# Scaling and splitting the attention weights: one scale per half matrix, maxima and the look for low halves on TensorE, and TensorE's program laid out twice

## The reference, cut to what matters

```python
x = x + attn(layernorm(x), wq, bq, wk, bk, wv, bv)   # x: 1 x 2048 x 1024
x = x + ffn(layernorm(x), w1, w2, w3)                # w1, w2: 2752 x 1024; w3: 1024 x 2752

def attn(h, ...):                                    # 32 heads of 32
    q = (h @ wq.T + bq).reshape(B, S, 32, 32)        # k, v alike; wq, wk, wv rounded to 8-bit floats (e4m3)
    scores = einsum('bshd,bstd->bsht', q, k) / sqrt(32)   # heads of one token against each other
    return einsum('bsht,bstd->bshd', softmax(scores), v).reshape(B, S, E)

def ffn(h, w1, w2, w3):
    dq = nf4_quant_dequant                           # blocks of 64, 16 levels
    return (silu(h @ dq(w1).T) * (h @ dq(w2).T)) @ dq(w3).T
```

## Time and profile before

| | us |
|---|---|
| median of 3 runs | 2055.94 (2054.3 to 2056.95) |
| profiled execution | 2054.98 |
| its span, first to last instruction | 2053.2 |

### The profile page before, as it was taken

How to read it: one execution, slowest core, us unless ns; L and a number is a source line. 1 busy time by engine, 2 the same in 40 slices (tenths; PEclk the granted TensorE clock), 3 DMA queues, 4 the chain that set the end, 5 groups by cost and what they waited for, 6 DMA issues and landing times. The chain is left out here.

```text
span 2053.2 us, 30858 instructions
## 1 busy us (share of the span) xinstructions
PE 1977.3 (96%) x10392; PEld 1069.7 (52%) x10392; DVE 1817.0 (88%) x1831; ACT 1466.1 (71%) x1640; POOL 1156.3 (56%) x700
## 2 busy tenths in 40 slices
PE   4699999999998999999999999999999999999998
PEld 3377878777776444444444444444444444444442
DVE  8679898998997899998989999899998989999972
ACT  5524242424256798989889899898998989898872
POOL 0100101010131669787787878878778796887964
PEclk8799999999997999999999999999999999999999
DMA  7114434343324651212122221212121212222114
GB/s 297 62 52 144 138 128 140 116 152 129 116 98 123 200 180 42 62 42 59 44 51 52 46 57 46 57 42 61 41 61 42 61 42 52 50 49 50 38 35 164
DMA packets 219661, 175.65 MB, mean 86 GB/s; under 512 B 143664, under 2 KB 186672, under 8 KB 219568
## 3 DMA queue, kind: packets, MB, share of 16 engines
q1 hardware_dynamic: 219568, 174.62, 29.4%
HBM read 115.34 MB, written 25.17 MB: 68 GB/s over the span
## 5 line engine op out<-in xcount | busy, mean ns | idle before, releaser
L1355 ACT ACTIVATE signs<-w_nat,compare_bias 128x1024 int8<-128x1024 f32 (+2 forms) x896 | 958.9, 1131 | 20.1 <-issue 17.8
L1482 DVE SCALAR_TENSOR_TENSOR bank<-signs,bank 128x1024 f32<-128x1024 int8 (+2 forms) x761 | 926.5, 1218 | 45.1 <-ACT signs L1355 16.4
L1655 PE MATMUL bank<-x2T_hi,w12T_hi 128*128 128x512 f16 x1376 | 521.5, 379 | 1.3 <-DVE w_nat L1499 1.3
L1656 PE MATMUL bank<-x2T_lo,w12T_hi 128*128 128x512 f16 x1376 | 521.5, 379 | 0.0
L1657 PE MATMUL bank<-x2T_hi,w12T_lo 128*128 128x512 f16 x1376 | 521.5, 379 | 0.0
L880 PE MATMUL bank<-wT_hi,xT_hi 128*128 128x512 f16 x768 | 293.0, 381 | 12.4 <-issue 12.4
L880 PE MATMUL bank<-wT_hi,xT_lo 128*128 128x512 f16 x768 | 292.9, 381 | 0.0
L1676 PE MATMUL bank<-w3T_hi,hT_hi 128*128 128x512 f16 x704 | 268.4, 381 | 13.4 <-DVE hidden L1508 7.4
L1677 PE MATMUL bank<-w3T_lo,hT_hi 128*128 128x512 f16 x704 | 267.7, 380 | 0.0
L1678 PE MATMUL bank<-w3T_hi,hT_lo 128*128 128x512 f16 x704 | 267.6, 380 | 0.0
L1283 POOL TENSOR_TENSOR acc<-acc,hidden 128x512 f32<-128x512 f32 x176 | 221.1, 1270 | 47.0 <-ACT hidden L1395 46.1
(11 more groups left out here) (126 smaller groups left out, 2720.6 us busy)
## 6 DMA issues: line engine op xcount, KB each, us to landing
ff_raw<-in_L_ffn_w SPq DMA_DIRECT2D x63, 512.0 KB, 4.5
w_nat<-in_L_ffn_w SPq DMA_DIRECT2D x63, 512.0 KB, 3.9
x_nat<-in_L_attn_hidden_states SPq DMA_DIRECT2D x16, 512.0 KB, 3.7
x_res<-in_L_attn_hidden_states SPq DMA_DIRECT2D x16, 512.0 KB, 4.5
x<-x_res SPq DMA_DIRECT2D x16, 512.0 KB, 2.9
acc<-x SPq DMA_DIRECT2D x4, 2048.0 KB, 8.2
out<-acc SPq DMA_DIRECT2D x16, 512.0 KB, 2.6
w_raw<-in_L_attn_wq SPq DMA_DIRECT2D x8, 512.0 KB, 7.1
```

The costliest lines, as they stand in the source:

```text
L1355: nc.scalar.activation(signs[0:rows, ring(v, k), 0:cols], w_nat[0:rows, v % SLOTS, 0:cols], ACT.Sign, scale=COMPARE[SUMMED[k]][0], bias=co ...
L1482: V.scalar_tensor_tensor(to, part, HALF_STEP[SUMMED[k]], before, ALU.mult, ALU.add).then_inc(sign_used, 1)
L1655: nc.tensor.matmul(dst, hi, x2T_hi[:, toks, c], start=c == 0, stop=False)
L1656: nc.tensor.matmul(dst, hi, x2T_lo[:, toks, c], start=False, stop=False)
```

## The change

The weight stage works by half matrices, six groups of four parts (512 output columns), each with a scale of its own, set one group ahead. The maxima of the parts are shared between VectorE (6 parts) and ScalarE (18 parts; it takes the sum of magnitudes, an upper bound of the maximum). The maximum over partitions is found by turning the column of 128 maxima into a row on TensorE (turn_top), reducing the row on VectorE (set_row), and spreading the two scales back to all partitions by a matmul with ones (spread_row). PSUM is used in three slots of two banks: one transposition unit is eight 128x128 blocks, one high half and one low half instruction has 1024 columns. The low halves are looked at by TensorE: each 128x128 block is multiplied by itself (square_lo, 192 matmuls added up in one bank), and the diagonal is reduced at the end. The residual's first load waits for the first projected half, GpSimd's clearings move into steps 0 and 1 behind 1/std, ScalarE waits for each where it first writes the cleared tile, and x and the biases are loaded after a third of the weights is turned, as before. TensorE's whole program behind the flag, the feed-forward stage included, stands twice: first the one without low halves, which the branch falls into when the flag is zero, then the one with them.

```diff
-                both(attend_tensor, feed_tensor, pe)
+                attend_tensor(pe, feed_tensor)
...
+        GROUPS = 6
+        top = sb("qkv_top", [P, GROUPS])
+        ones = sb("ones", [P, P])
+        scale_row = sb("scale_row", [1, 3, GROUPS])
+        scales = sb("scales", [P, 2, GROUPS])
+        w_scale, un_scale = scales[:, 0], scales[:, 1]
...
-        RING = 4
-        FILLS = C * 2
+        SLOTS = 3
+        PAIRS = C // 2
         PART = C // LOADS
-        LOOKS = {4 + k: k for k in range(LOADS)}
-        SCALE = 13
-        STATS, NORM = 4, 8
+        GROUP_PARTS = LOADS // 2
+        BY_VECTOR = ((0, 2), (0, 2), (3,), (3,), (), ())
+        by_scalar = [(g, j) for g in range(GROUPS) for j in range(GROUP_PARTS) if j not in BY_VECTOR[g]]
+        STATS_GROUP = 4
+        LO_SQUARES = 6
+        TOPS = 7
+        X_TURN = GROUPS * PAIRS % SLOTS * 2
+        def pair_of(n):
+            g, i = divmod(n, PAIRS)
+            m, half = divmod(g, 2)
+            return g, m, (slice(None), m, slice(2 * i, 2 * i + 2), slice(half * BANK, half * BANK + BANK))
+        def pair_banks(n):
+            return bank[:, n % SLOTS * 2:n % SLOTS * 2 + 2]
...
-                sp.wait_ge(w_turned, FILLS)
+                sp.wait_ge(w_turned, 2 * PAIRS)
...
-                for m in range(3):
-                    pool.wait_ge(local_max, m + 1)
-                    nc.gpsimd.partition_all_reduce(top_all[:, m:m + 1], top[:, m:m + 1], P, ALL_MAX).then_inc(global_max, 1)
+
                 inv_std(pool, 0)
-                pool.wait_ge(lo_sum_ready, 1)
-                nc.gpsimd.partition_all_reduce(lo_sum[:, 1:2], lo_sum[:, 0:1], P, ALL_MAX).then_inc(lo_known, 1)
...
+                def look(g):
+                    for j in BY_VECTOR[g]:
+                        wait_part(dve, g, j)
+                        nc.vector.tensor_reduce(part_max[:, g, j:j + 1], part_of(g, j), AX.X, ALU.max,
+                                                apply_absolute_value=True).then_inc(w_seen, 1)
+                def find_top(g):
+                    if BY_VECTOR[g]:
+                        dve.wait_ge(w_seen, sum(len(js) for js in BY_VECTOR[:g + 1]))
+                    dve.wait_ge(w_summed, sum(at <= g for at, _ in by_scalar))
+                    nc.vector.tensor_reduce(top[:, g:g + 1], part_max[:, g], AX.X, ALU.max).then_inc(local_max, 1)
+                def set_row(g):
+                    pow2, w_row, un_row = (scale_row[:, k, g:g + 1] for k in (2, 0, 1))
+                    dve.wait_ge(top_turned, g + 1)
+                    seq.mark(nc.vector.tensor_reduce(pow2, bank[0:1, TOPS, 0:P], AX.X, ALU.max))
                     seq.wait(dve)
+                    seq.mark(nc.vector.tensor_scalar(pow2, pow2, TINY, None, ALU.max))
                     seq.wait(dve)
+                    seq.mark(nc.vector.tensor_scalar(pow2.bitcast(I32), pow2.bitcast(I32), EXPONENT_BITS, None, ALU.bitwise_and))
                     seq.wait(dve)
+                    seq.mark(nc.vector.reciprocal(w_row, pow2))
+                    nc.vector.tensor_scalar(un_row, pow2, 2.0 ** -14 / X_SCALE, None, ALU.mult).then_inc(row_set, 1)
+                    seq.wait(dve)
+                    nc.vector.tensor_scalar(w_row, w_row, 2.0 ** 14, None, ALU.mult).then_inc(row_set, 1)
+                def set_scale(g):
+                    dve.wait_ge(row_spread, g + 1)
+                    nc.vector.tensor_copy(scales[:, :, g], bank[:, TOPS, P + 2 * g:P + 2 * g + 2]).then_inc(scale_set, 1)
+                look(0)
+                find_top(0)
+                set_row(0)
+                set_scale(0)
+                look(1)
+                for n in range(GROUPS * PAIRS):
+                    g, m, dst = pair_of(n)
+                    i = n % PAIRS
+                    if i == 0:
+                        dve.wait_ge(scale_set, g + 1)
+                    dve.wait_ge(w_hi_done, n + 1)
+                    nc.vector.scalar_tensor_tensor(wT_lo[dst], pair_banks(n), w_scale[:, g:g + 1], wT_hi[dst],
+                                                   ALU.mult, ALU.subtract).then_inc(w_lo_done, 1)
+                    if g + 1 < GROUPS and i < 3:
+                        (find_top, set_row, set_scale)[i](g + 1)
+                    if i == 2 and g + 2 < GROUPS:
+                        look(g + 2)
+                    if i == 3 and g == STATS_GROUP - 1:
+                        norm_stats(dve, 0, 0, 1)
+                    if i == 3 and g == STATS_GROUP:
+                        norm_apply(dve, 0, 0)
+                dve.wait_ge(lo_looked, 1)
+                seq.mark(nc.vector.tensor_tensor(lo_squares[:], bank[:, LO_SQUARES, 0:P], ident[:], ALU.mult))
+                seq.wait(dve)
+                nc.vector.tensor_reduce(lo_sum[:, 0:1], lo_squares[:], AX.X, ALU.max).then_inc(lo_sum_ready, 1)
+                dve.wait_ge(lo_added, 1)
+                nc.vector.tensor_copy(lo_sum[0:1, 1:2], bank[0:1, TOPS, 0:1]).then_inc(lo_known, 1)
+                split_lo(dve, 0, xT_lo[:, 0], xT_hi[:, 0], x_hi_done, x_lo_done, X_TURN)
...
-                def look_at_lo(q):
-                    act.wait_ge(w_lo_done, 2 * q + 2)
-                    if q > 0:
-                        act.wait_ge(lo_looked, q)
-                    nc.scalar.activation(lo_abs[:], wT_lo[:, q // C, q % C], ACT.Abs,
-                                         accum_out=lo_sums[:, q:q + 1]).then_inc(lo_looked, 1)
-                for m in range(3):
-                    act.wait_ge(scale_set, m + 1)
-                    for f in range(FILLS):
-                        n = m * FILLS + f
-                        c, half = f // 2, f % 2
-                        act.wait_ge(w_turned, n + 1)
-                        nc.scalar.activation(wT_hi[:, m, c, half * BANK:half * BANK + BANK], bank[:, n % RING],
-                                             ACT.Copy, scale=w_scale[:, m:m + 1]).then_inc(w_hi_done, 1)
-                        if half == 1 and n > 1:
-                            look_at_lo(n // 2 - 1)
-                split_hi(act, 0, xT_hi[:, 0], x_turned, x_hi_done)
-                look_at_lo(3 * C - 1)
+                def look(at):
+                    g, j = by_scalar[at]
+                    wait_part(act, g, j)
+                    if at > 0:
+                        act.wait_ge(w_summed, at)
+                    nc.scalar.activation(w_abs[:], part_of(g, j), ACT.Abs, accum_out=part_max[:, g, j:j + 1]).then_inc(w_summed, 1)
+                looked = 0
+                for n in range(GROUPS * PAIRS):
+                    g, m, dst = pair_of(n)
+                    while looked < len(by_scalar) and PAIRS * by_scalar[looked][0] - 7 + by_scalar[looked][1] <= n:
+                        look(looked)
+                        looked += 1
+                    if n % PAIRS == 0:
+                        act.wait_ge(scale_set, g + 1)
+                    act.wait_ge(w_turned, n + 1)
+                    nc.scalar.activation(wT_hi[dst], pair_banks(n), ACT.Copy, scale=w_scale[:, g:g + 1]).then_inc(w_hi_done, 1)
+                split_hi(act, 0, xT_hi[:, 0], x_turned, x_hi_done, X_TURN)
...
+                def square_lo(n):
+                    _, m, (_, _, cs, cols) = pair_of(n)
+                    for c in range(cs.start, cs.stop):
+                        for at in range(cols.start, cols.stop, P):
+                            lo = wT_lo[:, m, c, at:at + P]
+                            end = n == GROUPS * PAIRS - 1 and c + 1 == cs.stop and at + P == cols.stop
+                            done = nc.tensor.matmul(bank[:, LO_SQUARES, 0:P], lo, lo, start=n == 0 and c == 0 and at == 0, stop=end)
+                    if n == GROUPS * PAIRS - 1:
+                        done.then_inc(lo_looked, 1)
+                def turn_top(g):
+                    pe.wait_ge(local_max, g + 1)
+                    nc.tensor.transpose(bank[0:1, TOPS, 0:P], top[:, g:g + 1], ident[:]).then_inc(top_turned, 1)
+                def spread_row(g):
+                    pe.wait_ge(row_set, 2 * (g + 1))
+                    nc.tensor.matmul(bank[:, TOPS, P + 2 * g:P + 2 * g + 2], ones[0:1], scale_row[:, 0:2, g],
+                                     start=True, stop=True).then_inc(row_spread, 1)
+                pe.wait_ge(consts_set, 6 + LEVELS)
+                for n in range(GROUPS * PAIRS):
+                    g, m, _ = pair_of(n)
+                    i = n % PAIRS
+                    if n >= SLOTS:
+                        pe.wait_ge(w_lo_done, n - SLOTS + 1)
+                    for c in range(2):
+                        for j in range(GROUP_PARTS):
+                            if i == 0 and c == 0:
+                                wait_part(pe, g, j)
+                            last = nc.tensor.transpose(pair_banks(n)[:, c, j * P:(j + 1) * P],
+                                                       w_raw[m][:, g % 2 * GROUP_PARTS + j, (2 * i + c) * P:(2 * i + c + 1) * P], ident[:])
+                    last.then_inc(w_turned, 1)
```

(54 more changed lines are left out.)

87 lines of the change are left out of this document (20 added, 67 removed).

## The result

The changed kernel takes 2024.06 us (2023.24 to 2025.37, 4 runs) for 2055.6 (2054.3 to 2056.95, 4 runs): ratio 0.9852 [0.9832, 0.9872], 31.5 us faster. 2039 was forecast, 2031 to 2047 as the range: the direction held, the size was off by a factor of two. The profiled execution took 2023.94 us with a span of 2022.2. In the later runs two of 55 executions of before (2044.89 and 2046.10 us) and one of seven of d_pad90 (2035.71) are 10 to 13 us faster than the others of their kernel; none of the three was profiled, and why they are faster is open.

A forecast was written before the change was run, and what follows sets the result against it. TensorE, without slack behind the first projection, was taken as the bound, with 87.6 us ahead of it. 2054.98 - 18.3 (stage 14.0, branch 5.4, tail minus 1.1) + 2 = 2038.7, said as 2039 us; range 2031 to 2047.

The forecast's parts named there:

- The stage: Weight stage ahead of the first projection: last low half ends at 64.0 us for 77.99, 14.0 us of the gain.
- the walk through the groups: Weight stage's six groups at about 8.2, 8.2, 7.8, 9.0, 8.0 and 5.5 us, ending at 63.2 from 16.5.
- The squares: TensorE's look at low halves in the weight stage: 0.86 us per pair, weight loads half hidden.
- Behind the last low half: Weight stage's tail: flag at 66.7 us, block ends at 68.0, first projection at 69.3; new tail costs 1.1 us.
- The 2 us allowed for half clock in the stage: Weight stage: stretches with TensorE at half clock, where a pair costs 2.7 to 3.6 us, add 2 us.
- The restart: First projection's start: a full clock at once would give 2.6 us; bounds 0 and 2.6, taken as 0.
- The rest of the program: Everything behind the first projection: each step starts earlier by the same amount, about 16 to 18 us from 110 us on.
- the branch falls through: TensorE's test ahead of the first projection: 5713 ns falls below 300 ns, 5.4 us of the gain.
- the jump at the end: TensorE's jump over the second program copy at the program's end: costs 0 to 1 us, taken as 0.
- the wait on SyncE: Loads held until the first projected half: cost taken as 0, up to 3 us kept possible.
- rival of the first projection: TensorE bounds stage: 82 to 84 us, chance 0.15; branch costs as before: 0.12; half clock throughout: near 107 us, 0.04.
- nothing waits: GpSimd's clearings, taken as 7 us each, move behind 1/std; q_diag is clear 9 us behind the barrier, needed some 22.

The follow-up runs named there:

- d_pad90: The kernel before with 180 fulfilled waits (90 instructions) added at the start of ScalarE's weight stage; 2048.91 us (0.9953).
- h_nosq: The changed kernel with TensorE's squares of low halves left out for 23 of 24 pairs; 2023.16 us (0.985).
- c_pad38: The changed kernel with 76 fulfilled waits (38 instructions) added at the start of ScalarE's weight stage; 2032.63 us (0.9887).
- r_res: The changed kernel with the residual's load sent without the new wait for the first projection; 2024.31 us (0.9845).
- i_best: The changed kernel with two of ScalarE's looks given to VectorE and x's low halves made ahead of the flag; 2022.8 us (0.9849).
- l_pad60: The changed kernel with 120 fulfilled waits (60 instructions) added at the start of ScalarE's weight stage; 2024.08 us (0.9846).
- a_flip: The changed kernel with TensorE's program for low halves put first, so that the flag's test jumps again; 2028.26 us (0.9863).
- e_clear: The kernel before with only GpSimd's two clearings moved behind the second and third tile's 1/std; 2048.6 us (0.9967).
- f_twice_clear: The kernel before with TensorE's program doubled, so the branch falls through, and GpSimd's clearings moved behind 1/std; 2051.63 us (0.9984).
- j_tensor_flag: The kernel before with TensorE's program doubled and the flag reduced by a TensorE matmul and VectorE copy instead of GpSimd's all-reduce; 2049.16 us (0.9976).
- b_twice: The kernel before with only TensorE's program doubled, so that the test falls through; 2059.11 us (1.0014).
- p_pad1: The kernel before with two fulfilled waits (one instruction) added at the start of ScalarE's weight stage; 2050.39 us (0.9972).

## Why the forecast was half of the gain

The span gave 31.0 us, the forecast 16.3. The 14.7 missing, step by step:

1. **The stage, 64.0 forecast, 60.82 measured: 3.2 us.** The durations of the passes were right (high half 1.11 for 1.06, a run of low halves 4.89 / 4 = 1.22 for 1.20). Mis-sized was the walk through the groups: 8.2, 8.2, 7.8, 9.0, 8.0 and 5.5 us were forecast, 8.8, 7.6, 6.5, 7.9, 8.1 and 5.5 measured, so 2.4 of the 3.2 us are groups 2 and 3, and 0.8 is the rounding from 63.2 up to 64.0. The squares were mis-sized too: 0.86 us was taken for a pair, while the row shows eight in 0.61 with the pipeline's tail, and 16 in 1.06, 0.066 each, 0.53 for a pair; TensorE was busy for 36.1 us of the stage, not 43. That this made the stage shorter isn't shown: taking the squares away altogether gives 1.4 to 2.3 us (h_nosq), and most of that in groups 0, 1 and 4. The Trainium skill, TensorE: Matmul & The Clock Gate, section "What you observe", was named in the forecast for 56 ns and a stage 3 us shorter; the trace has 66 ns.
2. **Behind the last low half: 1.3 us.** 5.3 forecast, 64.83 - 60.82 = 4.0 measured: mostly squares again (the last ones end 0.7 us behind the last low half, for 1.4), and the fall-through at 90 ns.
3. **The 2 us allowed for half clock in the stage** weren't needed: it was at half for 3.4 us early on and full from 21.3 us to the end.
4. **The restart: 0.9 us.** Half clock for 3.4 us instead of 5.3, half of the difference; 0 had been taken inside the bounds 0 to 2.6. This term differs between executions: the clock fell to half for 3.4 us in after, c_pad38, h_nosq and r_res, and stayed full through the restart in i_best and l_pad60.
5. **The rest of the program: 7.3 us (7.5, less 0.2 of the attention part).** The sentence "every step behind the first projection therefore starts earlier by whatever the first projection starts earlier" failed. It rested on rows that end at 590 us and on the 96% of the whole span. The row behind them has 13.4 us in which TensorE is idle:

```profile
780.00:2053.20 1273.20, 1259.85 (x5800) 561.14 (x5798) 1146.67 (x1071) 1100.66 (x1209) 996.84 (x548) 1.00 0.23 54
```

In the last loop 0.75 us a round were idle time, and the profile had their source, 17.8 us of "issue" ahead of ScalarE's largest group and 60 packets on q14. Neither was read, and the instructions that the change takes out of ScalarE were costed only as time in the stage. c_pad38 and d_pad90 show what stands in the sentence's place: a round goes by ScalarE's pause behind the loop's branch, and that pause by where its code stands.

Right were: the branch falls through at almost nothing (its row is 5.6 us shorter than before; a jump in the changed kernel costs 4.2, a_flip), the jump at the end is hidden, the wait on SyncE costs nothing (r_res), and no rival of the first projection came about.

Right in size for a wrong reason was "nothing waits" for GpSimd. The forecast read the 7.17 us before the 1/std as clearings that last 7 us. They last 3.5; the pause belongs to the partition all-reduce ahead of them and the two MODIFY_POOL_CONFIG behind it, and it is there wherever the clearings stand (e_clear 10.25 us, f_twice_clear 11.53, none in j_tensor_flag or after). In the kernel before, the branch's gain was lost while the all-reduce stayed, with the clearings in either place: the doubled program made it 2.6 us slower (b_twice), and f_twice_clear, which is e_clear with the doubled program, is 3.0 slower than e_clear; in the changed kernel, whose 1/std would come as late, the same is to be expected, though no run has it with the all-reduce. That the gain of the branch depends on an edit of another part is what the sum had missed, and it was luck that the change makes that edit.

The far jumps and the reloads look like one family. Test and jump over the unused program took 5713, 3781 and 4079 ns here, the same test in place 90. The Trainium skill, Runtime: NRT & Kernel Launch, section "Instruction fetch mechanics", says that a taken branch to code outside the resident blocks waits for a load. The runs agree: ScalarE's 2.9 us behind a loop's branch come with loads and vanish with them. The Trainium skill calls the crossing of a block mostly hidden in that section, and the fifth load of a round in before, 68 us behind the branch, goes without a pause. A shift of the code thus seems to decide whether the branch finds its target loaded, which is worth 0.93 us a round. Why a shift by one lowers the pause from 2.9 to 2.5 us, and which places are good, stays open. Against its place in after, the loop stands 60 instructions further on in l_pad60 and 128 in d_pad90, which don't reload, and 38 in before and c_pad38 and 39 in p_pad1, e_clear and f_twice_clear, which make five loads a round.

## What to carry to other kernels

Before costing a change, read the instruction queues and the "issue" idle time at each loop's end: when a loop's length in TensorE time changes with a few instructions put ahead of it, place it first, and compare two kernels only with that accounted for. When a long stall is removed, list what it hid, here GpSimd's late 1/std, and check that each is ready earlier too. When an experiment's time comes out as expected, look whether the microseconds lie where they were expected: those of f_twice_clear did not. A reduction over partitions of a few numbers belongs on TensorE where GpSimd has work soon after and is waited for.

## What the runs showed of the hardware

- ScalarE's pause at the end of a loop of 272 instructions is 0.2 us or 2.4 to 3.4 us by where the loop stands; 76 fulfilled waits cost 8.5 us of 2024, 180 put into before gave back 7.6.
- GpSimd's next 1/std starts 10.6 us (e_clear) and 11.9 us (f_twice_clear) behind a partition all-reduce whose own row shows 0.38 us, and 14.8 us behind it with two clearings between, 7.2 of these idle. The clearings themselves aren't held (the first starts 0.3 us behind the all-reduce). Two MODIFY_POOL_CONFIG, 11 to 83 ns each, stand ahead of each such pause, and from them it is 5.7 to 11.1 us; what happens meanwhile no row shows.
- VectorE's normalisation of a 128x1024 tile takes 0.81 us by itself and 3.97 beside GpSimd's clearing of 128x4096 (after, e_clear and f_twice_clear alike).
- A jump over TensorE's unused program takes 3.7 to 5.8 us over all runs, and it is hidden where the engine still has queued matmuls (in after it lies from 2013.1 to 2017.2, the matmuls go on to 2016.9).
- 128x128 matmuls in 16 bits with fresh weights each follow each other at 0.066 us at the full clock.
